# Attention's first steps, K's sums and PV's shape in a fused attention and ternary layer on eight cores

## The reference

```python
x = x + attn(layernorm(x))
x = x + ffn(layernorm(x))

# attn
q, k, v = split(h @ Wqkv, 3)
q, k = rope(rmsnorm(q, q_norm_w)), rope(rmsnorm(k, k_norm_w))
mask = (q_idx >= k_idx) & (q_idx - k_idx <= 1023)
probs = softmax(where(mask, q @ k.T / sqrt(128), -inf))
out = (probs @ v) @ Wo

# ffn: entries are quantized to three values
x_q = ternary_quantize(h, 0.33, 0.5)
w   = ternary_quantize(weight, 0.2, 0.6) + rram_variation
out = einsum('bsd,od->bso', x_q, w)
```

## Time and profile before

| | |
|---|---|
| time, median of 3 runs | 1102.94 us (1102.21 to 1105.05) |
| profiled execution | 1100.83 us |
| its span, slowest core (core 3) | 1099.3 us |
| spans of the eight cores | 1093.7 (core 0), the others 1095.2 to 1099.3 us |
| mean granted clock of TensorE | 0.993 to 0.998 |
| TensorE busy | 1036.7 us, 94% |
| VectorE busy | 739.6 us, 67% |
| ScalarE busy | 454.6 us, 41% |
| GpSimd busy | 205.0 us, 19% |

### The profile page before, as it was taken

How to read it: one execution, slowest core, us unless ns; L and a number is a source line. 1 busy time by engine, 2 the same in 40 slices (tenths; PEclk the granted TensorE clock), 3 DMA queues, 4 the chain that set the end, 5 groups by cost and what they waited for, 6 DMA issues and landing times.

```text
span 1099.3 us, 20490 instructions; the slowest of 8 cores (1093.7 to 1099.3 us)
## 1 busy us (share of the span) xinstructions
PE 1036.7 (94%) x6796; PEld 546.7 (50%) x6796; DVE 739.6 (67%) x1286; ACT 454.6 (41%) x737; POOL 205.0 (19%) x222
## 2 busy tenths in 40 slices
PE   0899999999999999999999699999999899999998
PEld 0454444444444444444444466667666644444443
DVE  2783344588888764578886699999999666661311
ACT  1785333333333332221111699999999700000000
POOL 0012000000000000011000456656666500000000
PEclk9999999999999999999999899999999999999999
DMA  8986789755858767839101111554235272227322
GB/s 171 299 267 126 159 172 210 174 134 128 215 152 218 185 158 170 209 111 210 58 17 39 42 67 52 136 173 117 40 93 101 42 233 54 39 39 210 116 77 77
DMA packets 57386, 145.43 MB, mean 132 GB/s; under 512 B 21698, under 2 KB 25794, under 8 KB 53314
## 3 DMA queue, kind: packets, MB, share of 16 engines
q1 hardware_dynamic: 45858, 103.19, 30.3%
q0 software_dynamic: 11424, 40.90, 21.1%
HBM read 147.21 MB, written 26.21 MB: 158 GB/s over the span
## 4 chain that ended last, share of the span: by engine, by line
PE 78%; ACT 7%; issue 6%; DMA 5%; DVE 3%; ACTq 0%; POOL 0%; DVEq 0%; SPq 0%; POOLq 0%
PE ps L458 28%; PE ps L449 20%; PE ps L643 10%; PE ps L561 10%; ACT RW L739 3%; PE ps L585 3%; PE ps L530 3%; PE ps L599 2%; DVE RW L902 2%; DMA RC<-rrT 2%; DMA RW<-wqkv 2%; ACT sq L739 2%; PE ps L485 1%; ACT RC L745 1%; DMA RB<-x_all 1%
## 5 line engine op out<-in xcount | busy, mean ns | idle before, releaser
L458 PE MATMUL ps<-RA,RW 128*128 128x512 bf16 x1536 | 332.2, 379 | 0.9 <-ACT sq L707 0.9
L458 PEld LDWEIGHTS ps<-RA,RW 128*128 128x128 bf16 x1536 | 150.2, 98 | 182.4 <-issue 1.4
L449 PE MATMUL ps<-RW,RA 128*128 128x512 bf16 x1024 | 226.0, 381 | 0.0
L902 DVE TENSOR_SCALAR_CACHE_REDUCE RW<-ps 128x1152 f32<-128x1152 f32 x128 | 173.2, 1353 | 21.4 <-PE ps L533 15.0
L449 PEld LDWEIGHTS ps<-RW,RA 128*128 128x128 bf16 x1024 | 100.0, 98 | 118.6 <-issue 2.2
L419 POOL TENSOR_SCALAR RW<-RW,rinv 128x1152 bf16<-128x1152 bf16 x86 | 105.2, 1223 | 140.1 <-DVE rinv L916 139.6
L530 PE MATMUL ps<-RB,RC 128*128 128x512 bf16 (+1 forms) x384 | 109.0, 331 | 19.9 <-DVE RW L902 7.8
L846 DVE TENSOR_TENSOR ps<-ps,sq 128x512 f32<-128x512 f32 x90 | 62.6, 697 | 79.7 <-ACT sq L707 79.7
L561 PE MATMUL ps<-RB,RC 128*128 128x512 bf16 x512 | 111.2, 379 | 0.0
L739 ACT ACTIVATE RW<-RW,negm 128x1152 bf16<-128x1152 f32 x86 | 108.4, 1260 | 0.0
L704 ACT ACTIVATE RB<-ps,qkw_s 128x512 bf16<-128x512 f32 x64 | 44.0, 687 | 138.9 <-PE ps L458 136.0
(11 more groups left out here) (100 smaller groups left out, 1125.7 us busy)
## 6 DMA issues: line engine op xcount, KB each, us to landing
RW<-wqkv POOLq DMA_DIRECT2D x48, 512.0 KB, 11.6
RB<-x_all SPq DMA_DIRECT2D x16, 1024.0 KB, 7.2
RB<-wfT SPq DMA_DIRECT2D x22, 512.0 KB, 6.5
RB<-rrT SPq DMA_DIRECT2D x22, 512.0 KB, 8.5
RB<-wo POOLq DMA_DIRECT2D x16, 512.0 KB, 6.3
RA<-x_all SPq DMA_DIRECT2D x8, 1024.0 KB, 9.1
y<-sq SPq DMA_DIRECT2D x32, 256.0 KB, 2.6
ffhbm<-stg SPq DMA_DIRECT2D x14, 512.0 KB, 10.9
```

What stands on the lines that cost most here:

```text
L449: m = e.matmul(bank(g % 3), xlnT(d, 128 * t, 128), wslot(b)[:, 512 * d:512 * (d + 1)], start=(d == 0), stop=(d == 15))
L458: m = e.matmul(bank(g % 3), wslot(b)[:, 512 * d + 128 * hh:512 * d + 128 * (hh + 1)], xlnT(d, tok, 512), start=(d == 0), stop=(d == 15))
L902: e.tensor_scalar(out=sm(i), in0=scores(i), scalar1=-1.0, scalar2=None, op0=ALU.mult, op1=ALU.min, accum_out=negm[:, i % 4:i % 4 + 1]).the ...
```

## The change

Five things change. The lines of the changed kernel differ from those of before: L449 becomes L473 (V's groups), L530 and L533 become L553 and L556 (scores and masks), L585 becomes L602 (PV), L599 becomes L634 (transposes).

1. The branch moves from attention to the top: TensorE's whole program is now a function of `halo`, and each arm holds all of it.
2. V's last four groups (156 to 159) move into attention: one behind the first `s_wide` and `s_last`, one at the end of each of the loop's first three turns. They and the two before them use banks 5, 6 and 7 (`vbank`). ScalarE copies them behind its first four exponentials. The buffers `sm`, `prob` and `pT` move, so that they don't lie on the weights that these groups still read.
3. K's four sums are made in one go: two behind group 113, two behind group 114, where before one stood behind each of 115, 117, 119 and 121. Each root has a buffer of its own. VectorE's third and fourth `split` no longer wait for the store of the ternary weights out of `stg`.
4. PV takes two query tiles at once: for a pair of steps ten matmuls, eight of 256 columns and two of 128, in place of 18 of 128. The first five stand in the odd turn behind `s_wide`, the other five in the even turn ahead of it. `pT` has room for three pairs, and PV is one turn later on average.
5. VectorE copies six transposed tiles, ScalarE three, each as a strided piece of `pT`. ScalarE's copy of bank 7 comes one turn later (i % 4 is 0).

```diff
+    def vbank(g):
+        return bank({END - 6: 5, END - 5: 6, END - 4: 5, END - 3: 6, END - 2: 7, END - 1: 7}.get(g, g % 3))
...
-    ONESB = [5, 5, 5, 6, 7, 5]
+    ONESB = [5, 5, 5, 6, 7, 3]
...
+    def pT_place(m):
+        return (stg, 4096, 0) if m % 3 == 0 else (RW, 16384, 8192 + 2560 * (m % 3 - 1))
...
             def v_group(b, g, t):
-                bank_free(g)
+                if g < END - 6:
+                    bank_free(g)
+                elif g == END - 6:
+                    e.wait_ge(rms_std, 6)
+                elif g in (END - 4, END - 3):
+                    e.wait_ge(pj_free, g - 1)
+                elif g == END - 1:
+                    e.wait_ge(pj_free, g)
...
-                    if n in (115, 117, 119, 121):
-                        g = (n - 115) // 2
-                        sum_rows(2 + g, k_hl[2 * g:2 * g + 2])
+                        if n in (113, 114):
+                            for g in (2 * (n - 113), 2 * (n - 113) + 1):
+                                sum_rows(2 + g, k_hl[2 * g:2 * g + 2])
...
-            e.wait_ge(pj_free, END)
+                e.wait_ge(pj_free, END - 6)
...
+                def pv_part(m, tiles):
+                    p, j = divmod(2 * m, NQ)
+                    if 1 in tiles:
+                        e.wait_ge(t5_out, 2 * m + 2)
+                        e.wait_ge(t6_out, 2 * m + 2)
+                        if m in (16, 32, 48):
+                            e.wait_ge(v_back[m // 16 - 1], 16)
+                        if m % 2 == 0 and m >= 2:
+                            e.wait_ge(o_out, m // 2)
+                    for u in tiles:
+                        c0, c1 = (0, 128) if u == 0 else (128, 256) if u == 9 else (0, 256)
+                        o = 3584 + 256 * (m % 2)
+                        mm = e.matmul(ps[:, o + c0:o + c1], vtile(HEADS[p], j + u), pT_in(m, u), start=u == 1, stop=u == 8)
+                    if 8 in tiles:
+                        mm.then_inc(pv_mm, 2)
...
+                def attention():
+                    s_wide(0)
+                    s_last(0)
+                    s_wide(1)
+                    v_group(11, END - 4, NT - 4)
+                    for i in range(NSTEP + 5):
+                        if i + 1 < NSTEP:
+                            e.wait_ge(s_max, i + 1)
+                            s_last(i + 1)
+                        if i == 4:
+                            e.wait_ge(pj_free, END)
+                        if 6 <= i and i % 2 == 0:
+                            pv_part((i - 6) // 2, range(4, 9))
+                        if i + 2 < NSTEP:
+                            s_wide(i + 2)
+                        if 5 <= i < NSTEP + 5 and i % 2:
+                            pv_part((i - 5) // 2, (1, 0, 9, 2, 3))
...
+                        if i < 3:
+                            v_group(11, END - 3 + i, NT - 3 + i)
...
             with e.If(has_halo == 0):
-                attention(False)
+                program(False)
...
-                    e.copy(pT(n)[:, 640:1152], bankb(6, 512)).then_inc(t6_out, 1)
+                    e.copy(pT_out(n, 6, 3), bankb(6, 384).rearrange("p (l c) -> p l c", l=3)).then_inc(t6_out, 1)
...
-                if i >= 7 and i % 4 == 3:
-                    qd = (i - 7) // 4
+                if i < 4:
+                    v_evac(END - 4 + i)
+                if i >= 8 and i % 4 == 0:
+                    qd = (i - 8) // 4
...
-            e.wait_ge(ff_spill[1], 16 * 7)
+            e.wait_ge(q_spill[0], 16 * 4)
             split(4, KACC[2], k_hl[4:6])
...
-                    e.tensor_copy(out=pT(n)[:, 0:640], in_=bankb(5, 640)).then_inc(t5_out, 1)
+                    e.tensor_copy(out=pT_out(n, 0, 6), in_=bankb(5, 768).rearrange("p (l c) -> p l c", l=6)).then_inc(t5_out, 1)
```

More of the change, by code:

```diff
@@ L187, in sm @@
     def sm(n):
-        c = 4672 + 1152 * (n % 2)
+        c = 640 + 1152 * (n % 2)
         return RW32[:, c:c + 1152]
@@ L631, in _ @@
-            for c in range(4):
-                for j in range(NQ):
-                    n = NQ * c + j
-                    if c == 0:
-                        e.wait_ge(xq_T[j % 2], 16 * (j // 2 + 1))
-                    if j == 0:
-                        e.wait_ge(ff_back[c], 16)
-                    if 4 <= n < 8:
-                        e.wait_ge(x2_out, 25 + n)
-                    elif n >= 8:
-                        e.wait_ge(y_res, n - 7)
-                    for d in range(16):
-                        m = e.matmul(bank((n + 4) % 8), qT(d, 128 * j, 128), ffw(c, d), start=(d == 0), stop=(d == 15))
-                    m.then_inc(ff_mm, 1)
+                program(True)
@@ L659, in v_evac @@
                 dst = vstg(g) if g < V3 else RC[:, 8192 + 512 * (g - V3):8192 + 512 * (g - V3 + 1)]
-                e.copy(dst, bank(g % 3)).then_inc(pj_free, 1)
+                e.copy(dst, vbank(g)).then_inc(pj_free, 1)
             for t in range(NT + VLAG + 1):
@@ L711, in _ @@
                     rms_root(1, q_root[1], 1.0 / 16.0, 128.0 * RMS_EPS)
-            for g in range(V1, END):
+            for g in range(V1, END - 4):
                 if g == V3:
```

301 lines of the change are left out of this document (149 added, 152 removed).

## The result

The changed kernel took 1097.47 us (median of 8), the kernel before 1103.42 beside it. The ratio is 0.9949 [0.9938, 0.9961]: 0.5% faster, some 6 us. The forecast was 1088.8 us, its range 1085.0 to 1096.8. So the sign was right, and the time lies 0.7 us outside of the range, 8.7 from the forecast. The profiled execution took 1097.34 us at a span of 1095.8; it was the slowest core, core 3, that was shown, as before. Against the profiled span of before, 1099.3, that is 3.5 less.

The account below looks back on a forecast made before the run. It took TensorE's groups up to V's end, a jump of some 4 us, then attention's ring of 1.98 us a step as bounds. Gains of 10.3 (head) and 3.8 (steps) made 14.1: 1102.94 to 1088.8 us, range 1085.5 to 1091.

Parts of the forecast that it names:

- What has to be ready is VectorE: End of K's ropes: VectorE, finished at 596.65 before, is wanted at 591.7 and must come 5 us earlier through K's sums.
- The latest start: K's tables on VectorE: they start at 458.8 at the latest, 449.5 by the sums, once root and cosines are there.
- The term of 10.3 for the head: V's end and attention's first steps: step 4's reduction starts at 608.3 in place of 618.54; gain 10.3 us.
- Rival C: Head: no overlap, since cosines land late or groups wait for ScalarE; some 4 us less, 1093; chance 0.10 with E.
- The term of 3.8 for the steps: Attention steps 4 to 127: mostly 1.98 us each, 245.4 in place of 249.2; gain 3.8 us.
- the place of PV against bank 7's copy: Attention's odd turns: PV wants bank 7 0.49 us later, so its 0.27 us wait for ScalarE's copy goes.
- Rivals A: Attention: the long steps stay and only the head gains 10.3 us, giving 1092.6; chance 0.15.
- B: Attention: VectorE's longer copy becomes the bound, a step is 1.98 + 0.064; gain 6.1 us, 1096.8; chance 0.12.
- D: Attention: six tiles come too late every turn, a step is 2.19 us; slower at 1112.8 us; chance 0.04.
- rival E: Branch: the jump's 4 us appear elsewhere on the path, say from both arms being long; 1093; chance 0.10 with Rival C.
- TensorE's stall of 0.7: K's sums at their new place: TensorE stalls 0.7 us, between 0 and 3.5, as the first sum runs.
- if nothing came earlier: K's sums: if nothing came earlier from them, TensorE would wait some 2.5 us at `s_last(1)`.

Follow-up runs that it names:

- kernel 1: The changed kernel with VectorE's last four ternary units six ropes later, in ropes 14 to 17: 1088.49 us, ratio 0.9870.
- kernel 4: The changed kernel with the weights of V's third quarter (block 10) issued six groups later: 1096.17 us, ratio 0.9933.
- kernel 8: The kernel before with only the last four ternary units moved to ropes 14 to 17: 1101.46 us, ratio 0.9994.
- kernels 9: The changed kernel with ternary units and block 10's weights later, plus PV's odd-turn half put directly behind the last scores: 1088.13 us, ratio 0.9876.
- kernel 11: The changed kernel with ternary units and block 10 later, PV's odd half behind the last scores, and tiles copied five and four: 1088.50 us, ratio 0.9885.
- kernel 10: The changed kernel with ternary units and block 10 later, plus five transposed tiles copied by VectorE and four by ScalarE: 1086.11 us, ratio 0.9860.
- kernel 2: The kernel before with only the branch moved to the top: 1102.42 us, ratio 0.9995.
- kernel 12: The changed kernel with ternary units and block 10 later, plus block 9's weights three groups of K later: 1084.47 us, ratio 0.9843.
- kernel 7: The changed kernel with ternary units in ropes 14 to 17 but K's sums at their old places: 1093.44 us, ratio 0.9923.

## Why the prediction was wrong, point by point

**The step that failed** is the one that says "What has to be ready is VectorE", and in it "They start when root and cosines are there, at 449.5 by the sums and at 458.8 at the latest, and end at 468 to 478. The ropes' end moves to 583 to 592.3." Two things were wrong in it.

- The latest start was taken from the kernel before, from a wait for a root. That wait hid another: the first sines had landed at 456.8, only 2.0 us ahead of it. In the changed kernel they landed at 459.9, and the tables start at 460.05 (at 455.8 to 462.5 on kernel 1's cores). A row that names one releaser bounds that one alone. This error was small, and not where the time went: kernel 1's tables end no earlier (477.8 for 478.0) and its head is as counted, and 10 us earlier bring 0.6 us.
- From the tables to the ropes' end I added the old distance, as if only VectorE's work lay in it. It also held the loads for four ternary units. Their queue follows TensorE's groups (V's last weights) as well as VectorE. So when VectorE comes earlier, its loads don't, and on core 3 they came later. A wait of 0.55 became 9.46. Kernel 1 gives the head's 9 us back, and kernel 4 shows that VectorE's earliness alone turns into this wait.

Another step cost 2.9 us and had no term in the sum, that V's second quarter starts where it did, at 436.06 on core 3. It starts 2.9 us later on average. In that are 1.2 of Q's later start, 1.2 of a longer wait for ScalarE's square ahead of K's last group (1.4 us on average, for 0.3), and 0.4 of slow clock behind it (on cores 3 and 6). The forecast took all that stands ahead of V as unchanged, the jump's new place included.

**The term of 10.3 for the head** is then 0.9 in the changed kernel by the means (181.9 to 181.0) and 9.6 in kernel 1. TensorE's part of it (17.66 from the last four groups to step 4, no wait for copies between the groups) was right to a few tenths. Rival C, "VectorE comes no earlier because the cosines land late", was the right kind of failure at the wrong load, and it was priced at 4 us. Its price left out what the wait does to the clock: 6.09 us of idle time made the next group 2.02 longer.

**The term of 3.8 for the steps** was right in its mechanism as a whole and in its size on the core that it was read from: 249.18 to 244.95 on core 3. It was low for this profile, since cores 1, 2 and 4 had taken 251.7 to 252.0 before (every fourth step 2.21 in place of 2.13), which I hadn't looked at. The mean gain is 5.3, and 4.4 against kernel 8, which has the same attention and no core with the longer step. Of the cause I had claimed, the place of PV against bank 7's copy, kernels 9 and 11 bear out 1.4 to 2.5 us of it on cores 1 to 7. How it acts is less clear: on core 3 the profile gives that copy 1.4 us of PV's idle time in kernel 9 and 5.6 in kernel 11, and the steps of kernel 11 are the shorter ones. The copy of six and three is worth nothing (kernel 10). The rest, 2 to 3 us, goes with PV in pairs itself: five matmuls now stand ahead of the transposes where nine stood. That fits the 5.5 us of wait in kernel 11 that no longer lengthen the turn much, but no run took the pairs back alone, nor ScalarE's copy of bank 7 to its old turn, so it is argued and not shown. Rivals A, B and D are refuted: next to no long steps, no step longer by the copy, no late transposes. That B's time, 1096.8, lies near the measured one is chance.

**The branch.** That the hole at V's end goes is shown by kernel 2 (3.7 us less from V's start to step 4, the "issue" gone). At the program's start, on core 3 before and after:

```profile
19.73 1.86 PE L485 MATMUL ps<-ident,RB 128*128 128x128 bf16 x16 [19.73 <-ACT RB L676]
...
30.07 1.87 PE L485 MATMUL ps<-ident,RB 128*128 128x128 bf16 x16 [8.48 <-ACT RB L676]
```

```profile
25.29 1.86 PE L508 MATMUL ps<-ident,RB 128*128 128x128 bf16 x16 [25.29 <-issue]
...
30.68 1.86 PE L508 MATMUL ps<-ident,RB 128*128 128x128 bf16 x16 [3.52 <-ACT RB L717]
```

TensorE's first transposes start at 24 to 25 on cores 1 to 7 instead of at 19 to 20, its next ones at 30.0 on average instead of 29.0. So the jump moved under the first loads, as forecast, but not quite for nothing: in all 12 profiles with the branch on top the next ones start at 29.5 to 30.4 (means of cores 1 to 7), in the two without it at 29.0, and on core 0 no later than before. The Trainium skill says the like in "Runtime: NRT & Kernel Launch", section "Instruction fetch mechanics": a taken branch to a target outside the current pages makes the engine wait for a fetch. It gives no price; here it is the 4.13 of the earlier trace rows. What isn't settled is how much of V's later start this makes. With the branch on top Q's first group starts at 101.5 to 102.8 (means of 12 profiles), without it at 101.4 and 101.6, so 0 to 1.4 us may be the price at the new place. That would be rival E, at some 1 us and not at 4. The rest is the wait for ScalarE's square. ScalarE had waited for VectorE, and VectorE for the piece at 429.30 (7.25 us, 6.66 in the kernel before); kernel 12 shows that this can be taken away.

**K's sums.** TensorE's stall of 0.7 was forecast right: in the changed kernel it is 0.54 to 0.56 on six of the eight cores, ahead of the second sum, and absent on cores 3 and 6, where V started last. The price "if nothing came earlier" (2.5 us of waiting) was too low: in kernel 7 TensorE waits 4.0 there, and the head is 5.3 longer.

**The account.** The means of before and after differ by -5.3 in the steps, -0.9 in the head, and +2.9 in V's start; the end of attention gives 0.5 (last reduction to the first product of Wo 4.04 for 4.53 on core 3). That is -3.8, near the -3.5 of the two profiled spans; the medians differ by 6.0, since the profiled execution of before (1100.83) was a fast one. The forecast had -3.8, -10.3, nothing and nothing. So the head missed by 9.4 and V's start by 2.9, and the steps and the end gave 2.0 back.

## What to carry to other kernels

When an engine is to come earlier, list what else it consumes between the point where it gets faster and the point where it is wanted, and for each load ask which engine's progress issues it: a load that is issued by another engine's progress doesn't come along. A wait in the profile names only the last releaser, so bound the second one by its own landing time before you price the first as gone. And price a wait of the tensor engine in the middle of its stream with what follows it: here 6 us of waiting cost 8, 4 cost 5 to 6, and up to 1.3 cost only themselves.

## What the hardware showed that I had not expected

- One move of four small units among VectorE's ropes was worth 9 us in one kernel and nothing in another (kernels 1 and 8). The edit was free of work in both.
- From issue to landing a load of 512 KB took 14.1 us behind 2 MB of weights whose issue had begun 8 us before, and 22.2 right behind them, on the same queue; a store of 512 KB in the same stretch 7.2 and 16.2. Issuing it earlier brought nothing: it landed 2.5 and 2.9 us behind the weights.
- ScalarE's and VectorE's copies of transposed tiles could be shifted by a tile with no effect on the step (244.5 and 244.6), though VectorE was busy for nearly all of it (92% of 608 to 872 us in the kernel before).
- The cores of one program had two lengths of the long step before (2.13 and 2.21; 249.2 to 249.7 and 251.7 to 252.0 in all), and another execution of the same attention (kernel 8) had only the shorter one; with the new order all but core 0 agree within 0.2 us (244.9 to 245.1).
